# Last mixture of a two-layer network: split-precision down product, feature-major output and one pipeline over all experts

## The reference

```
logits = x @ router_W + router_b
w, idx = top_k(logits, 2);  w = softmax(w);  gates = one_hot(idx, 8) . w
xhat = (x - mean) * rsqrt(var + 1e-5)
h = xhat * ln_g[e] + ln_b[e]
a = gelu(h @ W1[e] + b1[e])          # 128 -> 512, exact gelu
y = a @ W2[e] + b2[e] + x            # 512 -> 128
out = sum_e gates[e] * y
```

## Time and profile before

| | us |
|---|---|
| median of 3 runs (2453.78 to 2456.22) | 2454.6 |
| the profiled execution, its own time | 2461.0 |
| its span, first to last instruction | 2459.2 |
| PE busy in the span | 2072.9 (84%) |
| DVE busy | 1628.2 (66%) |
| ACT busy | 999.3 (41%) |
| POOL busy | 666.7 (27%) |
| the last stage, from its first instruction to the end | 1968.2 to 2459.2 |

### The profile page before, as it was taken

How to read it: one execution, slowest core, us unless ns; L and a number is a source line. 1 busy time by engine, 2 the same in 40 slices (tenths; PEclk the granted TensorE clock), 3 DMA queues, 4 the chain that set the end, 5 groups by cost and what they waited for, 6 DMA issues and landing times. The chain is left out here.

```text
span 2459.2 us, 46736 instructions
## 1 busy us (share of the span) xinstructions
PE 2072.9 (84%) x16920; PEld 1647.0 (67%) x16920; DVE 1628.2 (66%) x4182; ACT 999.3 (41%) x1990; POOL 666.7 (27%) x409
## 2 busy tenths in 40 slices
PE   3888888884899989999768874899689879999998
PEld 2677777663566645665557763788477768888887
DVE  5777777775877738776477777677667774333344
ACT  1455555552255543555422222233233233444443
POOL 3555555553155542555300004000300010000000
PEclk9999999996699987999879997899799969999999
DMA  4111111111000000000000001000000020000000
GB/s 155 70 70 66 68 63 64 64 61 36 1 1 1 1 1 1 1 1 1 1 1 0 0 0 42 1 1 1 1 1 1 1 79 5 4 4 4 4 4 9
DMA packets 34795, 54.88 MB, mean 22 GB/s; under 512 B 7104, under 2 KB 16960, under 8 KB 33856
## 3 DMA queue, kind: packets, MB, share of 16 engines
q1 hardware_dynamic: 34624, 52.57, 5.9%
HBM read 16.90 MB, written 2.10 MB: 8 GB/s over the span
## 5 line engine op out<-in xcount | busy, mean ns | idle before, releaser
L1047 POOL TENSOR_TENSOR mb_psum<-mb_pt 128x1024 f32<-128x1024 f32 x112 | 267.0, 2387 | 313.3 <-ACT mb_pt L1027 312.4
L1027 ACT ACTIVATE mb_pt<-mb_stb 128x1024 f32<-128x1024 f32 x256 | 249.1, 1020 | 147.1 <-PE mb_stb L1128 146.6
L2328 PEld LDWEIGHTS md_bk<-md_w,md_a 128*128 128x128 f32 x2048 | 265.1, 192 | 27.3 <-ACT md_a L2175 4.2
L2175 ACT ACTIVATE md_a<-md_bk,md_b 128x512 f32<-128x512 f32 x256 | 175.5, 687 | 246.0 <-PE md_bk L66 245.7
L915 DVE TENSOR_REDUCE mb_mxp<-mb_p1b 128x1 f32<-128x512 f32 x352 | 231.2, 684 | 65.7 <-PE mb_p1b L1112 61.8
L2328 PE MATMUL md_bk<-md_w,md_a 128*128 128x128 f32 x2048 | 268.8, 276 | 4.0 <-DVE md_acc L2272 2.9
L2272 DVE SCALAR_TENSOR_TENSOR md_acc<-md_bk,md_gate,md_acc 128x128 f32<-128x128 f32 x256 | 71.8, 343 | 237.1 <-PE md_bk L2328 237.1
L351 DVE TENSOR_TENSOR ma_tr<-ma_pbank,ma_cs 128x512 f32<-128x512 f32 x256 | 161.7, 683 | 91.8 <-PE ma_pbank L66 81.7
L1951 ACT ACTIVATE mc_p<-mc_sb,mc_nb 128x512 f32<-128x512 f32 (+3 forms) x160 | 98.0, 621 | 189.1 <-DVE mc_nb L1839 189.1
L488 ACT ACTIVATE ma_e<-ma_sbank,ma_mx 128x80 f32<-128x80 f32 x512 | 120.4, 385 | 98.4 <-DVE ma_mx L358 98.4
L2029 PE MATMUL mc_pv<-mc_v,mc_pt 128*128 128x128 f32 x1088 | 150.1, 282 | 11.7 <-DVE mc_pt L1888 11.4
(11 more groups left out here) (329 smaller groups left out, 4884.9 us busy)
## 6 DMA issues: line engine op xcount, KB each, us to landing
ma_swp<-ma_tr SPq DMA_DIRECT2D x256, 128.0 KB, 2.0
mg_X<-x SPq DMA_DIRECT2D x4, 512.0 KB, 11.5
ma_cs<-cs SPq DMA_DIRECT2D x1, 2048.0 KB, 9.6
mc_cs<-cs SPq DMA_DIRECT2D x1, 2048.0 KB, 8.1
md_raw<-d_w SPq DMA_DIRECT2D x1, 2048.0 KB, 7.3
md_w<-d_w SPq DMA_DIRECT2D x1, 2048.0 KB, 10.9
out<-mg_X SPq DMA_DIRECT2D x8, 256.0 KB, 2.3
ma_raw<-w_qkv SPq DMA_DIRECT2D x1, 1536.0 KB, 9.7
```

The source lines that it names most:

```text
L1027: nc.scalar.activation(pt[:, T % RING, :, :].rearrange("p (b h) q -> p b (h q)", b=2), stb[:, 2 * (i % 2):2 * (i % 2) + 2, :], ACT.Exp, sc ...
L1047: nc.gpsimd.tensor_tensor(psum[:, n % SUMS, :, :], pt[:, T % RING, :, :], pt[:, (T + 1) % RING, :, :], ALU.add).then_inc(summed, 1)
L2175: nc.scalar.activation(a[:, e % 2, c, :], ub[:, c, :], ACT.Gelu, bias=b1[:, e, c:c + 1]).then_inc(gelu, 1)
L2328: last = nc.tensor.matmul(db[:, e % 2, s * P:(s + 1) * P], a[:, e % 2, c, s * P:(s + 1) * P], w2[:, e, c, :], start=(c == 0), stop=(c == F ...
```

## The change

The loop over blocks is unrolled into 64 items (block, expert) that follow one another, and the blocks' ends are laid into the items of the next block.

- **Down product.** W2 is loaded into `late`, rounded to `w2h` by ACT (eight copies) and its rest `w2l` made by POOL (eight subtractions), after the first part. W2 is now the stationary operand and the Gelu's output the moving one, both in two parts, so a down is again a triple of 512 columns, and its output `db[j % 2]` is feature-major.
- **Splitting `a`.** ACT writes the Gelu to `a`; `high` copies it to fp32r `ah` (three of four on ACT, the fourth on DVE, line 2358); `low` on DVE makes `al = a - ah` (line 2352).
- **Gates.** With features on the partitions the gate is a vector along the tokens. PE transposes the gates of a block, ACT copies them to SBUF, SP writes them to device memory (`d_gates`) and reads, for every item, one row of 512 gates spread over 128 partitions into one of four buffers `gb`. DVE's `scale` (line 2372) computes (db + b2) * gb, b2 a scalar per feature. POOL adds the result to `accT` (line 2269), for seven of eight experts.
- **End of a block.** PE transposes `accT` back (`turn_back`), DVE adds `xi * gsum` and makes the statistics and the result in 13 parts, two places per item, from the third expert of the next block on. SP stores a block about two blocks later.
- `FinishNorm` is used in its form by rows, which is already there for the third stage (lines 1489 to 1508).

The core of the diff:

```diff
-        w2 = m.sb("w2", [P, NE, FC, D])
+        w2h = m.sb("w2h", [P, NE, FC, D], F32R)
+        w2l = m.sb("w2l", [P, NE, FC, D], F32R)
...
+        ah = m.sb("ah", [P, FC, BLK], F32R)
+        al = m.sb("al", [P, FC, BLK], F32R)
...
+        late = m.sb("late", [P, NE, FF])
+        w2raw = late.rearrange("p e (c d) -> p e c d", d=D)
+        gb, accT, tmp = late[:, 0:GB, :], late[:, GB:GB + 2, :], late[:, GB + 2:GB + 4, :]
+        a = raw[:, 0:FC, :]
+        xi, acc = (raw[:, FC + k, :].rearrange("p (s d) -> p s d", d=D) for k in range(2))
+        gT = raw[0:NE, FC + 2:FC + 4, :]
+        F = FinishNorm(m, by_rows=True)
...
+                sp.dma_start(w2raw[:, :, :, :], dr["d_w2"]).then_inc(w2_in, 16)
+                sp.wait_ge(w2_lo, NE)
...
+                def keep_gates(n):
+                    sp.wait_ge(gT_done, n + 1)
+                    sp.dma_start(dr["d_gates"][n], gT[:, n % 2, :]).then_inc(gT_out, 16)
+
+                keep_gates(0)
+                for j in range(ITEMS):
+                    n, e = divmod(j, NE)
+                    if e == 0:
+                        sp.wait_ge(gT_out, 16 * (n + 1))
+                    if j >= GB:
+                        sp.wait_ge(scaled, j - GB + 1)
+                    sp.dma_start(gb[:, j % GB, :], dr["d_gates"][n, e].partition_broadcast(P)).then_inc(gb_in[j % GB], 16)
+                    if e == KEEP_AT and n + 1 < NBLK:
+                        keep_gates(n + 1)
+                    if e == STORE_AT[1] and n >= STORE_AT[0]:
...
+                act.wait_ge(w2_in, 16)
+                for e in range(NE):
+                    nc.scalar.activation(w2h[:, e, :, :], w2raw[:, e, :, :], ACT.Copy).then_inc(w2_hi, 1)
...
+                def hidden(j, c):
+                    e = j % NE
+                    act.wait_ge(up_mm, j * FC + c + 1)
+                    if j >= 1:
+                        act.wait_ge(lo_done, (j - 1) * FC + c + 1)
+                    nc.scalar.activation(a[:, c, :], ub[:, c, :], ACT.Gelu, bias=b1[:, e, c:c + 1]).then_inc(gelu, 1)
+
+                def high(j, c):
+                    act.wait_ge(gelu, j * FC + c + 1)
+                    if j >= 1:
+                        act.wait_ge(down_mm, (j - 1) * FC + c + 1)
+                    nc.scalar.activation(ah[:, c, :], a[:, c, :], ACT.Copy).then_inc(hi_act, 1)
...
+                turn_gates(0)
+                for j in range(ITEMS):
+                    n, e = divmod(j, NE)
+                    hidden(j, 0)
+                    hidden(j, 1)
+                    high(j, 0)
+                    hidden(j, 2)
+                    high(j, 1)
+                    hidden(j, 3)
+                    high(j, 2)
...
+                for e in range(NE):
+                    pool.wait_ge(w2_hi, e + 1)
+                    nc.gpsimd.tensor_tensor(w2l[:, e, :, :], w2raw[:, e, :, :], w2h[:, e, :, :].bitcast(F32),
+                                            ALU.subtract).then_inc(w2_lo, 1)
+                for j in range(ITEMS):
+                    n, e = divmod(j, NE)
+                    if e > 0:
+                        pool.wait_ge(scaled, j + 1)
+                        if e > 1:
+                            pool.wait_ge(added, n * (NE - 1) + e - 1)
+                        nc.gpsimd.tensor_tensor(accT[:, n % 2, :], accT[:, n % 2, :], tmp[:, e % 2, :],
+                                                ALU.add).then_inc(added, 1)
+                    if e == POWER_AT[1] and n >= POWER_AT[0]:
+                        F.pool(nc, pool, n - POWER_AT[0], S)
...
-                with dve.Fori(0, NBLK) as n:
...
+                def low(j, c):
+                    dve.wait_ge(gelu, j * FC + c + 1)
+                    if c < HIA:
+                        dve.wait_ge(hi_act, j * HIA + c + 1)
+                    else:
+                        dve.wait_ge(hi_dve, j + 1)
+                    nc.vector.tensor_tensor(al[:, c, :], a[:, c, :], ah[:, c, :].bitcast(F32), ALU.subtract).then_inc(lo_done, 1)
+
+                def high(j, c):
+                    dve.wait_ge(gelu, j * FC + c + 1)
+                    if j >= 1:
+                        dve.wait_ge(down_mm, (j - 1) * FC + c + 1)
+                    nc.vector.tensor_copy(ah[:, c, :], a[:, c, :]).then_inc(hi_dve, 1)
+
+                def scale(j):
+                    n, e = divmod(j, NE)
+                    dve.wait_ge(down_mm, (j + 1) * FC)
+                    dve.wait_ge(gb_in[j % GB], 16 * (j // GB + 1))
+                    if e == 0:
+                        if n >= 2:
+                            dve.wait_ge(turned, n - 1)
+                        dst = accT[:, n % 2, :]
+                    else:
+                        if j >= 3:
+                            dve.wait_ge(added, n * (NE - 1) + max(e - 2, 0))
+                        dst = tmp[:, e % 2, :]
+                    nc.vector.scalar_tensor_tensor(dst, db[:, j % 2, :], b2[:, e:e + 1], gb[:, j % GB, :], ALU.add,
+                                                   ALU.mult).then_inc(scaled, 1)
+
...
+                def total(n, s):
+                    tile = n * BPT + s
+                    dve.wait_ge(ln, tile + 1)
+                    dve.wait_ge(turned, n + 1)
+                    nc.vector.scalar_tensor_tensor(acc[:, s, :], xi[:, s, :], gsum[:, tile:tile + 1],
+                                                   fb[:, s * P:(s + 1) * P], ALU.mult, ALU.add).then_inc(row_sum, 1)
...
+                def finish_at(t):
+
+                    n, part = divmod(t - FINISH_AT, 2 * NE)
+                    if 0 <= n < NBLK and part < PARTS:
+                        finish(n, part)
+
+                for j in range(ITEMS):
+                    low(j, 0)
+                    low(j, 1)
+                    finish_at(2 * j)
+                    high(j, 3)
+                    low(j, 2)
+                    if j > 0:
+                        scale(j - 1)
+                    low(j, 3)
+                    finish_at(2 * j + 1)
...
-                with pe.Fori(0, NBLK) as n:
...
+                def down(j, c):
+                    n, e = divmod(j, NE)
+                    if c == 0:
+                        if n == 0:
+                            pe.wait_ge(w2_lo, e + 1)
+                        if j >= 2:
+                            pe.wait_ge(scaled, j - 1)
+                    if c < HIA:
+                        pe.wait_ge(hi_act, j * HIA + c + 1)
+                    else:
+                        pe.wait_ge(hi_dve, j + 1)
+                    pe.wait_ge(lo_done, j * FC + c + 1)
+                    matmul_split(nc, db[:, j % 2, :], w2h[:, e, c, :], w2l[:, e, c, :], ah[:, c, :], al[:, c, :],
+                                 start=(c == 0), stop=(c == FC - 1)).then_inc(down_mm, 1)
+
+                def turn_back(n):
+                    pe.wait_ge(added, (n + 1) * (NE - 1))
+                    if n > 0:
+                        pe.wait_ge(row_sum, n * BPT)
+                    for s in range(BPT):
+                        last = nc.tensor.transpose(fb[:, s * P:(s + 1) * P], accT[:, n % 2, s * P:(s + 1) * P], ident[:, :])
+                    last.then_inc(turned, 1)
...
+                for c in range(FC):
+                    up(0, c)
+                turn_gates(0)
+                for j in range(ITEMS):
+                    n, e = divmod(j, NE)
                     for c in range(FC):
-                        up(0, c)
-                    for e in range(NE):
-                        for s in range(BPT):
-                            if e + 1 < NE:
-                                up(e + 1, s)
-                            down(e, s)
-                    pe.wait_ge(gelu, (n + 1) * NE * FC)
-                    pe.wait_ge(acc_done, n * NA + NA)
+                        if j + 1 < ITEMS:
+                            up(j + 1, c)
+                        if c == 2 and e == GATE_AT and n + 1 < NBLK:
+                            turn_gates(n + 1)
+                        if c == 2 and e == 1 and n > 0:
+                            turn_back(n - 1)
+                        down(j, c)
+                turn_back(NBLK - 1)
```

More of the change, by code:

```diff
@@ L2077 @@
 FC = FF // P
+GB = 4
+GATE_AT = 3
+KEEP_AT = 7
+STORE_AT = (2, 6)
+POWER_AT = (1, 4)
+APPLY = (10, 12)
+FINISH_AT = 2 * (NE + 2)
 def ffn_layer1(nc, dr, X, g, out):
@@ L2131, in ffn_layer1 @@
         ln = m.sem("ln")
+        w2_in = m.sem("w2_in")
+        w2_hi = m.sem("w2_hi")
+        w2_lo = m.sem("w2_lo")
         up_mm = m.sem("up_mm")
         gelu = m.sem("gelu")
+        hi_act = m.sem("hi_act")
+        hi_dve = m.sem("hi_dve")
+        lo_done = m.sem("lo_done")
         down_mm = m.sem("down_mm")
-        acc_done = m.sem("acc_done")
+        scaled = m.sem("scaled")
+        added = m.sem("added")
+        gT_mm = m.sem("gT_mm")
+        gT_done = m.sem("gT_done")
+        gT_out = m.sem("gT_out")
+        gb_in = [m.sem(f"gb_in{k}") for k in range(GB)]
+        turned = m.sem("turned")
+        row_sum = m.sem("row_sum")
```

(23 more changed lines are left out.)

101 lines of the change are left out of this document (41 added, 60 removed).

## The result

| | median of the runs | own time of the profiled execution | its span |
|---|---|---|---|
| before, same chip | 2455.41 (2453.78 to 2456.25, 4 runs) | | 2459.2 |
| after | 2413.26 (2412.15 to 2415.43, 4 runs) | 2415.43 | 2413.6 |

The ratio is 0.983 [0.9813, 0.9847]: 42.2 us, or 1.7%, faster. The forecast was 2402.0 within 2390 to 2425.

A forecast was written before the change was run, and what follows sets the result against it. PE was taken to bound the kernel. Loop -71.4, later start +9.4, low clock +2.0 and longer end +7.4 gave -52.6 us: a median of 2402.0, range 2390 to 2425.

The forecast's parts named there:

- main theory: Last stage: PE sets the pace with cheaper triples and no seams; 2402 us, own range 2396 to 2410, chance 0.56.
- rival in which DVE and POOL set the pace: Expert loop: DVE, held up by POOL's adds, needs more per expert than PE; 2410 to 2450 us, chance 0.24.
- the start: Before the loop's first down: PE waits for gate sum, transposes, copies and Gelus, so the loop starts 9.4 us later.
- The clock term: Loop's start: PE, having been idle, begins at the low clock level; 2 us added.
- the lead: Expert loop: products are ready some 1.8 us ahead of the triple that reads them.
- waits just in time: Expert loop: each triple waits for ACT or DVE; 0.10 us per triple cancels the gain; chance 0.08.
- signs named beforehand: Loop trace: PE idle before a down with DVE's subtraction or cast as releaser means port rival; ACT means lead too short.
- port rival: Expert loop: POOL's adds hold up DVE at the shared port, so both set the pace; 2410 to 2450 us, chance 0.24.
- The tail: From the last down to the span's end: 17.1 us instead of 9.7, 7.4 more.
- The hold-up: Expert loop: POOL's add delays DVE by 1.11 us per expert on average, 0.28 of it beside useful work.
- it just fits: Expert loop: DVE's need with POOL's hold-ups, 5.47 us per expert, stays within PE's 5.58.
- Less lost at the ends: Start and end: each costs 3 us less and the clock recovers at once; 2394 us, chance 0.12.

The follow-up runs named there:

- e3: The changed kernel with POOL's add cut to 8 of 512 columns, the rest of the sum left out: 2411.3 us.
- e1: The changed kernel with PE's transposes of the next block's gates moved from behind the third up to behind the first: 2409.0 us.
- e2: The changed kernel with ACT's eight W2 copies, and so POOL's eight subtractions, moved earlier under the first layer norm: 2406.6 us.
- e4: The changed kernel with the low x high matmul left out of each down product, two matmuls instead of three: 2379.4 us.
- e5: The changed kernel with both cuts: down product without its low x high matmul, POOL's add on 8 of 512 columns: 2355.5 us.
- e6: The changed kernel with every POOL add done twice, the first into a spare tile: 2441.6 us.
- e10: The kernel of e8 with a block's second pair of results applied one part earlier (11, not 12): 2400.9 us.
- e8: The changed kernel with earlier gate transposes, earlier W2 splitting, and the first expert started ahead of the first gates' transposes: 2395.5 us.

## Why the prediction was right, and where it missed

**The range held, the main theory's own did not.** The median of 2413.3 lies within 2390 to 2425, but outside the 2396 to 2410 that the main theory had been given, and inside the 2410 to 2450 of the rival in which DVE and POOL set the pace. That rival isn't what happened: with POOL's add all but gone (e3) the loop is 0.3 us shorter. The mechanism in the loop was right; the start was priced too low and a seam in every block not at all, 11 us together.

**The bound was read rightly.** PE sets the pace before and after, a triple costs 0.697 us, and ten in a row show it. The loop was forecast at 360.6 us and 2 more for the clock. With the seam of the gate rows gone, as in e1, it takes 362.1. (The sum priced 14 groups of transposes at 0.45 us where its own row gives 0.49; by a block of e1, 45.45 us less 64 triples at 0.697, a group costs 0.42.) The clock term measured 1.9 in after: three triples took 2033.98 - 2030.01 = 3.97 us, not 2.09, after PE had been idle for 16.1 of the 18.8 us ahead of them, with this granted clock of 0.51, the 1.2 GHz level (busy time by stretch):

```profile
2030.00:2034.00 4.00, 3.99 (x10) 3.17 (x11) 2.33 (x4) 2.87 (x6) 0.00 (x0) 0.51 0.54 198
```

The 3.4 us from which the term was guessed are the stretch 2128.40 to 2131.79 in the trace of before, of which the earlier trace rows show a part. The gate transfers were hidden as said; nothing waits for them. The single table load held too.

**First missed term: the start, by 5.4 us.** The sum had the first down at 2026.9 when before's stage start is kept, 58.6 us behind that start, and it came at 64.0. The collision of POOL's subtractions with the router was in the working, "up to 1.3", and was given half a microsecond. It cost 5.3, which is 4.9 of the miss once the later gate sum is counted against that half; the other 0.5 lies in the steps from the gate sum to the first down, 6.2 us (2023.83 to 2030.01) for 5.6. The error is in the unit: 1.3 us is what *one* DVE operation can lose to one POOL operation, and here five stood in a row against eight, each losing nearly all of POOL's 1.23: (4.70 - 0.48)/4 = 1.05, and 1.12. e2 shows the cause: with the subtractions elsewhere the sum comes at 53.0, not 57.9. A look at the DVE operations of before that follow the scaling of W1 would have found five of the two-operand form.

**Second missed term: the seams, by 5.1 us** of the 5.4 that the loop was longer; the last 0.3 wasn't traced. The working treated ACT as hidden by its total, 4.2 of 5.58 us, and listed the seven Gelus and copies of an expert. The one operation that a block adds, the copy of the gate rows, costs only 0.59 us. It costs more by where it stands: it waits in order for PE, and PE's transposes stand behind three more ups. The prediction priced the transposes on PE but didn't name who is queued behind the wait that they release. ACT's idle 25% was no help, as the hole came at one place and the lead, 1.8 us by the forecast, was shorter than the wait of 3.4. This is the "waits just in time" rival in small: 0.73 us at seven of the 508 triples, not 0.10 at each. The signs named beforehand would have misled here. PE idle before a down with DVE's subtraction as the releaser was to mean the port rival, and that is the very row at 2055.22; e1 and e3 show that it is ACT's order and not POOL.

**The tail, 1.5 us better than the sum.** Each row took 2402.03 to 2403.30, 1.27 us, for 1.5, and applying a tile 2407.37 to 2407.96, 0.59, for 0.71 (timeline of the tail).

```profile
2402.03 0.18 DVE L1493 BATCH_NORM_AGGREGATE md_fmv<-md_fst 128x2 f32<-128x6 f32 x1 [0.15 <-DVE md_fst L1491]
...
2403.30 0.18 DVE L1493 BATCH_NORM_AGGREGATE md_fmv<-md_fst 128x2 f32<-128x6 f32 x1 [0.15 <-DVE md_fst L1491]
...
2407.37 0.35 DVE L1504 TENSOR_SCALAR md_raw<-md_raw,md_fmv,md_frs 128x128 f32<-128x128 f32 x1 [1.12 <-POOL md_frs L1512]
2407.75 0.29 DVE L1508 TENSOR_TENSOR mg_X<-mg_X,md_raw 128x128 f32<-128x128 f32 x1
2407.96 0.34 DVE L1504 TENSOR_SCALAR md_raw<-md_raw,md_fmv,md_frs 128x128 f32<-128x128 f32 x1
```

Why the 0.71 of the earlier trace rows was longer wasn't looked into. The three pieces, start +5.4, loop +5.4 and tail -1.5, are the 9.3 us between the forecast gain of 52.6 and the 43.3 of the stage; the medians show 42.2, and the last microsecond isn't resolved.

**DVE was less loaded than said.** Near 90% was named as a sign, and it was 81%. The cast took 0.42 us for 0.5. The hold-up was priced at 1.11 - 0.28 = 0.83 us per expert, and e4 against e5 gives 0.31. Most adds do meet a subtraction (40 of 56), but most of these lose only part of POOL's operation: 19.5 us in all in after, 0.5 per add that hits. The verdict "it just fits" came out right with a need of at most 5.33 us, not 5.47, and e6 shows that the rival's mechanism was real and near.

The Trainium skill, page "SBUF — State Buffer", section "Who interferes with whom", gives a rule for such hold-ups: the ports that DVE and GpSimd share go to one instruction as a whole, and a DVE operation asks for them with two SBUF inputs or in a two-port mode, which `tensor_scalar` can enter. The trace agrees that a DVE operation with two SBUF inputs is held (4.70 us for four). It also agrees that `tensor_scalar` is held (e2's 11.60 us and e10's 1.31); whether it ran in that mode no run here shows.

**Less lost at the ends** had a chance of 0.12. The end was 1.5 us better and the start 5.4 worse. That e8 came near that time, 2395.5, is the work of three further edits and doesn't speak for this rival.

## What to carry to other kernels

An engine with a quarter of its time idle isn't hidden if one instruction of its queue waits in order for another engine: for every wait, compare its length with the lead of the pipeline, not its duration with the idle share. Where two engines share a port, count the operations that stand against each other, as each can lose nearly a whole operation of the other (1.05 of 1.23 us here), however small it is itself. And when a wait's releaser is an engine that was itself idle, follow the releasers back until one was busy or misplaced; the edit belongs there (one digit in e1).

## What the hardware showed beyond expectation

The cost of a hold-up didn't depend on the size of the held operation: 128x32 operations lost 1.05 us (the mean of four additions) and 1.12 (a subtraction) beside POOL operations of 1.23, and a 128x512 subtraction up to 1.1 (the longest of L2352 took 1.79 us, against 0.69 with POOL's add cut). Scalings of 128x128 with per-partition scalars were held too: sixteen took 11.60 us beside POOL and 4.18 without. And an f32 matmul of 512 columns cost 0.85 us where three single-pass ones cost 0.70, so splitting the product pays 0.15 us on PE per triple even at equal width, for a subtraction of 0.69 us and a copy of 0.61 on other engines.
